# Six attentions make their scores twice, the second time with keys on the partitions

## What is computed

```python
# L0_attn, L2_attn: heads of 8, causal (L0 with rotary positions)
scores = q @ k.T / sqrt(8); scores = where(tril, scores, -inf); o = softmax(scores) @ v
# L1_xattn: heads of 8, 77 keys from the context, no mask;  L3_ffn: heads of 8, no mask
# L2_xattn = two attentions with heads of 32: a1 (128 keys) and a2 (77 keys of the context)
a = softmax(q @ k.T * 32 ** -0.5)
if causal: a = a * (arange(t)[None, :] > arange(s)[:, None])   # a1 only, AFTER the softmax
o = a @ v
```

## Time and profile before

| | us |
|---|---|
| median of 3 runs | 4947.15 |
| lowest, highest | 4937.4, 4949.03 |
| the profiled execution, span from its first to its last instruction | 4969.4 |

### The profile page before, as it was taken

How to read it: one execution, slowest core, us unless ns; L and a number is a source line. 1 busy time by engine, 2 the same in 40 slices (tenths; PEclk the granted TensorE clock), 3 DMA queues, 4 the chain that set the end, 5 groups by cost and what they waited for, 6 DMA issues and landing times.

```text
span 4969.4 us, 84778 instructions
## 1 busy us (share of the span) xinstructions
PE 4410.3 (89%) x29077; PEld 2535.4 (51%) x29077; DVE 2640.3 (53%) x6880; ACT 2593.2 (52%) x9813; POOL 836.2 (17%) x1454
## 2 busy tenths in 40 slices
PE   7888989989999999989799888998889888898796
PEld 3544764444454454448355444454455454554493
DVE  5555225655655655645454656556664565546523
ACT  4556434454454454453555556555655566555542
POOL 0111420011011011035021021110131021210350
PEclk9999989999999999999899989999999999999897
DMA  5000540000000000007000000000000000000172
GB/s 198 11 11 11 172 128 18 12 7 28 12 7 28 12 7 18 6 22 222 22 22 10 5 5 24 14 10 1 6 23 14 9 6 10 10 1 1 46 230 76
DMA packets 107750, 183.05 MB, mean 37 GB/s; under 512 B 13344, under 2 KB 69408, under 8 KB 107200
## 3 DMA queue, kind: packets, MB, share of 16 engines
q1 hardware_dynamic: 92544, 147.48, 9.9%
q0 software_dynamic: 13632, 28.04, 1.6%
q10 hardware_dynamic: 1152, 2.10, 0.1%
HBM read 126.33 MB, written 51.23 MB: 36 GB/s over the span
## 4 chain that ended last, share of the span: by engine, by line
PE 65%; DVE 20%; ACT 7%; issue 5%; DMA 2%; POOL 1%; SPq 0%; DVEq 0%; POOLq 0%; ACTq 0%
PE bank L713 8%; PE bank L866 7%; PE bank L883 6%; DVE rowmax L1693 6%; PE bank L745 4%; PE bank L1041 3%; PE bank L733 3%; PE bank L1152 3%; PE bank L1141 3%; PE bank L1023 3%; PE bank L790 3%; DVE probsT L1759 2%; PE bank L922 2%; PE bank L852 2%; ACT work L1323 2%
## 5 line engine op out<-in xcount | busy, mean ns | idle before, releaser
L1323 ACT ACTIVATE work<-bank,rowmax 128x128 f32<-128x128 f32 (+1 forms) x3072 | 1061.1, 398 | 208.6 <-DVE rowmax L1693 208.6
L1693 DVE TENSOR_REDUCE rowmax<-bank 128x4 f32<-128x512 f32 (+2 forms) x1152 | 614.0, 578 | 433.4 <-PE bank L866 314.8
L713 PE MATMUL bank<-mask_causal,identb 128*128 128x512 bf16 x2839 | 803.1, 394 | 22.6 <-DVE qd L1628 8.7
L883 PE MATMUL bank<-ident,work 128*128 128x128 f32 (+1 forms) x4096 | 641.0, 282 | 155.6 <-DVE probsT L1759 116.7
L1323 ACT ACTIVATION_READ_ACCUMULATOR work<-bank,rowmax 128x1 f32 x3072 | 753.1, 245 | 0.0
L883 PEld LDWEIGHTS bank<-ident,work 128*128 128x128 f32 (+1 forms) x4096 | 481.8, 144 | 377.7 <-DVE probsT L1759 196.8
L1759 DVE COPY probsT<-bank 128x512 f32<-128x512 f32 (+2 forms) x832 | 482.0, 601 | 55.3 <-PE bank L883 53.9
L713 PEld LDWEIGHTS bank<-mask_causal,identb 128*128 128x128 bf16 x2839 | 273.5, 101 | 290.7 <-issue 115.5
L866 PE MATMUL bank<-km,q 32*128 32x512 f32 (+2 forms) x1792 | 403.7, 562 | 1.9 <-issue 1.9
L2206 POOL TENSOR_TENSOR qd<-work 128x256 f32<-128x256 f32 (+1 forms) x64 | 64.7, 1012 | 1902.9 <-ACT work L1321 1836.5
L1257 ACT ACTIVATE part<-bank,eps 128x512 f32<-128x512 f32 x232 | 157.7, 680 | 383.8 <-PE bank L745 383.3
(11 more groups left out here) (336 smaller groups left out, 6902.5 us busy)
## 6 DMA issues: line engine op xcount, KB each, us to landing
slot<-in_w_L_ffn SPq DMA_DIRECT2D x78, 578.0 KB
slot<-in_w_stream SPq DMA_DIRECT2D x41, 512.0 KB
expert_rows<-slot SPq DMA_DIRECT2D x36, 516.0 KB, 6.3
slot<-in_w_L_ffn SPq DMA_DIRECT2D x39, 450.0 KB
qd<-expert_rows SPq DMA_DIRECT2D x117, 129.0 KB
back<-pair_rows SPq DMA_DIRECT2D x24, 512.0 KB, 5.3
slot<-in_w_stream SPq DMA_DIRECT2D x16, 256.0 KB
pair_rows<-qd,dest POOLq DMA_INDIRECT x234
```

Source lines behind the costliest of these rows:

```text
L713: nc.tensor.matmul(b[:], identb[:], mask["causal"][:].unsqueeze(1).to_broadcast([P, 4, P]), start=True, stop=True)
L883: ins = nc.tensor.transpose(b[0:nk, j * P:(j + 1) * P], probs[t % 2][:, r, j, 0:nk], ident[:])
L1323: ins = nc.scalar.activation(out, raw, ACT.Exp, bias=top, accum_out=expsum[t % 2][:, 4 * r + j:4 * r + j + 1])
L1693: V.tensor_reduce(m[:, 4 * r:4 * r + J], banks.where(("scores", n, c, s, r))[:, 0:J * nk] .rearrange("p (j k) -> p j k", j=J), AX_X, ALU.m ...
```

## The change

Six attentions (`KEYED`) get functions of their own, `keyed_mha`. The scores with queries on the partitions now serve the maxima alone. The negative maxima of an item, 16 columns, are split into two bf16 parts (value and remainder), laid out in `tops` and turned by one matmul. The scores are made a second time with keys on the partitions, and a matmul with a 0/1 weight (`top_pick`) adds each query's negative maximum to them in the bank. One exponential per block then gives `probsT` directly; nothing is turned. The sums come from matmuls with weights of ones (`totals`), already spread over the features; ScalarE inverts them by logarithm and exponential. In `L2_a1` the late mask is multiplied into a copy of `probsT` (in `probs`), blocks 0 and 1 by VectorE, 2 and 3 by GpSimd. Rings: `first` (banks 0 to 2) and `second` (3 to 5). `after_mask` becomes bf16, `average64` goes (the narrower variance is scaled in the logarithm), two small constants come in, `xcol` shares memory with `lcol`.

```diff
+KEYED = ("L0_attn", "L1_xattn", "L2_attn", "L2_a1", "L2_a2", "L3_ffn",)
+FRONT_ROWS, BACK_ROWS = (0, 1), (2, 3)
...
         banks = Banks(psum, {"flow": range(8), "scores": (0, 1, 2, 3), "turned": (4, 5), "attend": (6,), "wide": (7,),
-                             "head": (4, 5)})
+                             "head": (4, 5), "first": (0, 1, 2), "second": (3, 4, 5)})
...
+            # TensorE
+            def half(t, rows):
+                back = BACK_ROWS if rows == FRONT_ROWS else FRONT_ROWS
+                if t < GROUP:                               # (waits for q, k at s == 0)
+                    for r in rows:
+                        b = bank(("scores", n, c, s, r), ("row_max", (n, c, s, r)), "first")
+                        if st["mask"]: # identity x mask, 4 * nk columns bf16
+                if 1 <= t <= GROUP:                         # c, s = items[t - 1]
+                    for r in back:
+                        b = bank(("keyed", n, c, s, r), ("probsT", (n, c, s, r)), "second")
+                        if st["mask"]: # mask x identity, 512 columns bf16
+                for j in range(4):
+                    # scores of t: D == 32 one matmul of nk columns per r in rows; else at j == 0 one of 4 * nk
+                    # keyed of t-1: per r in back one matmul, keys x queries, 128 columns, stop=False
+            def turn_tops(t): # bank "first"; waits tops; one matmul tops x identb
+            def shift(t, rows):
+                if rows == BACK_ROWS:
+                    pe.wait_ge(*have("tops_taken", (n, c, s)))
+                for j in range(4):
+                    for r in rows:  # top_pick[g32, j] spread over nk x topsT[g32], 128 columns bf16, into keyed
+            def totals(t): # bank "wide", freed by log_sum; waits probsT of all r; 16 matmuls of 128 columns fp32
+            for t in range(GROUP + 2):
+                if t == GROUP + 1: step(then)
+                if t == 0: warm(6, "second")
+                half(t, FRONT_ROWS)
+                if 1 <= t <= GROUP: turn_tops(t - 1)
+                if t >= 2: totals(t - 2)
+                elif t == 1: warm(4, "second")
+                if 1 <= t <= GROUP: shift(t - 1, BACK_ROWS)
+                half(t, BACK_ROWS)
+                if 1 <= t <= GROUP: shift(t - 1, FRONT_ROWS)
+                # hooks of second; step(late[0]); attend(t - 2), in L2_a1 after kept_v, kept_p; output
+            # ScalarE, round t: take_tops(t - 1), soften(t - 1), invert(t - 2)
+            def soften(t):
+                for r in BACK_ROWS + FRONT_ROWS:
+                    act.wait_ge(*have("keyed", (n, c, s, r)))
+                    nc.scalar.activation(probsT..., banks.where(("keyed", n, c, s, r))..., ACT.Exp).then_inc(*made("probsT", (n, c, s, r)))
+            def invert(t): # waits summed; Ln from the bank -> log_sum; Exp(-1 x) -> inverse
+            # VectorE
+            for t in range(GROUP + 2):
+                if t < GROUP: row_max(t, FRONT_ROWS)
+                if st["post"] and t >= 2: keep_before(t - 2)   # probs = probsT * after_mask, r = 0, 1
+                if t >= 3: context(t - 3)
+                if t < GROUP:
+                    row_max(t, BACK_ROWS)
+                    split_tops(t)                              # two small steps
+                # hooks, late steps; at GROUP + 1 context(t - 2); add_residual
+            # GpSimd, L2_a1: the same product for r = 2, 3
```

More of the change, by code:

```diff
@@ L477, in decoder @@
         spreadT = [sb(f"spreadT{i}", [P, 4, P]) for i in range(2)]
+        tops = sb("tops", [P, P], BF16)
+        topsT = sb("topsT", [P, P], BF16)
         diag = [B["y"][c][:, 0:PER * 32].rearrange("p (s i) -> p s i", s=PER) for c in C]
@@ L547, in _ @@
                 nc.gpsimd.memset(onesb[:], 1.0)
+                nc.gpsimd.memset(tops[:], 0.0)
                 nc.gpsimd.memset(slots[SLOTS - 1][:], 0.0)
@@ L567, in _ @@
                 nc.vector.memset(wmean[:], 0.0)
-                nc.vector.memset(average64[:], 1.0 / CTX_DIM)
                 for value, t in eps.items():
@@ L668, in norm_rings, with keyed, top_cols @@
             return "flow", "flow"
+        def keyed(st):
+            return untagged(st["name"])[0] in KEYED
+        def top_cols(part):
+            return tops[:].rearrange("p (r x) -> p r x", r=4)[:, :, 0:8] \
+                .rearrange("p r (j i) -> p r j i", i=2)[:, :, :, part]
         def summed_by_pool(st, r):
-            return not st["linear"] and not st["mask"] and r in POOL_SUMS
+            return not st["linear"] and not st["mask"] and not keyed(st) and r in POOL_SUMS
         def per_feature(st):
@@ L744, in variance @@
                     pe.wait_ge(*have("squared", (n, c)))
-                    nc.tensor.matmul(b[0:rows, 0:w], (average if rows == P else average64)[:],
+                    nc.tensor.matmul(b[0:rows, 0:w], average[0:rows, 0:rows],
                                      B["sq"][c][0:rows, 0:w],
@@ L817, in mha @@
                 def mha(st, second, then):
+                    if keyed(st):
+                        keyed_mha(st, second, then)
+                        return
                     n, nk, D = st["name"], st["nk"], st["D"]
@@ L1300, in mha_head, with keyed_mha, take_tops @@
                     yield
+                def keyed_mha(st, second, then):
+                    n, nk, D = st["name"], st["nk"], st["D"]
+                    def take_tops(t):
+                        c, s = items[t]
+                        act.wait_ge(*have("tops_turned", (n, c, s)))
+                        nc.scalar.activation(topsT[:], banks.where(("tops_turned", n, c, s))[:, 0:P],
+                                             ACT.Copy).then_inc(*made("tops_taken", (n, c, s)))
+                    def soften(t):
+                        c, s = items[t]
+                        if t >= 2:
+                            act.wait_ge(*have("attended", (n, *items[t - 2])))
+                        for r in BACK_ROWS + FRONT_ROWS:
+                            act.wait_ge(*have("keyed", (n, c, s, r)))
+                            nc.scalar.activation(probsT[t % 2][0:nk, r, :, :], banks.where(("keyed", n, c, s, r))[0:nk, :]
+                                                 .rearrange("p (j t) -> p j t", j=4),
+                                                 ACT.Exp).then_inc(*made("probsT", (n, c, s, r)))
+                    def invert(t):
+                        c, s = items[t]
+                        w = 4 if D == 32 else 1
+                        out = spreadT[t % 2][:, 0:w, :]
+                        if t == 0 and untagged(n)[0] == "L2_a1" and st["group"]:
+                            for i in C:
+                                act.wait_ge(*have(f"scattered{i}", (tagged("L3_route", st["group"] - 1), i, 1, PER - 1)))
+                        if t >= 2:
+                            act.wait_ge(*have("context", (n, *items[t - 2])))
+                        act.wait_ge(*have("summed", (n, c, s)))
+                        nc.scalar.activation(out, banks.where(("summed", n, c, s))[:, 0:w * P].rearrange("p (i t) -> p i t", i=w),
+                                             ACT.Ln, scale=float(P) if D == 32 else 1.0).then_inc(*made("log_sum", (n, c, s)))
+                        act.wait_ge(*have("log_sum", (n, c, s)))
+                        nc.scalar.activation(out, out, ACT.Exp, scale=-1.0).then_inc(*made("inverse", (n, c, s)))
+                    for t in range(GROUP + 2):
+                        if 1 <= t <= GROUP:
+                            take_tops(t - 1)
+                            soften(t - 1)
+                        if t >= 2:
+                            invert(t - 2)
+                        for _ in range(st["hooks"].count(t)):
+                            step(second)
+                        if t == st["drained"]:
+                            drain(second)
+                        if t:
+                            step(late[0])
+                        if t == PER + 1 and untagged(n)[0] == "L3_ffn":
+                            g = st["group"]
+                            for c in C:
+                                act.wait_ge(*input_of(("normed", tagged("L3_xattn_ln", g)), c))
+                                act.dma_start(io["kept"][:, (g * CHAINS + c) * TOK:(g * CHAINS + c + 1) * TOK], B[st["src"]][c][:]
+                                              ).then_inc(*made(f"kept{c}", (g, c), 16))
+                        if t == GROUP + 1:
+                            step(then)
+                            step(then)
```

221 lines of the change are left out of this document (216 added, 5 removed).

## The result

The changed kernel takes 5186.35 us in the median (5156.61 to 5190.27, 4 runs) against 4948.09 for the kernel before in the same comparison: ratio 1.0464, 95% interval 1.0428 to 1.0499. It is slower by 4.6%, where 4915 and a gain were forecast. The profiled execution has a span of 5184.5 us against 4969.4.

A forecast was written before the change was run, and what follows sets the result against it. TensorE, busy 89% of the span, was taken as the bound. Six attentions -55 us, moved wait +22, setup under 0.5: sum -32, span 4969 to 4937; the median, 22 us below the span, gives 4915 us, range 4800 to 5045.

The forecast's parts named there:

- TensorE's round: TensorE's time for one round of a keyed attention: 5.9 us unmasked, 7.2 us masked.
- the halves: In each round, scores and the previous item's keyed scores run beside each other on different row groups, 1.0 us a half.
- the wait for the fourth bank: TensorE idles after the first shift until ScalarE's exponential frees the first block's bank: 0.95 us, only 0.2 in masked items.
- the count's wait: In six masked attentions the routing's count waits for bank `wide` behind ScalarE's logarithm: 1.8 us twice in each, +22 us.
- rival E: Idle time lets TensorE's clock fall to 1.2 GHz in 13 of 128 unmasked rounds: +63, 4978 us; chance 0.05.
- removed fillers and turns: Taken out of TensorE's round: sixteen turns (1.75 us of slots) and all fillers between turns (up to 1.3 us).
- C's middle: Rival C, slower halves: each 0.1 us more costs 38 us, 5049 us at 1.35, 5299 fully serial; chance 0.15.

The follow-up runs named there:

- split: Changed kernel with half of the totals issued behind the back shift in unmasked keyed attentions: 5141.73 us, 1.0232 of the kernel before.
- Experiments 1 to 3 and 7 to 9: fill77; changed kernel's 77-key stages with 128 key columns, 1.0444; tall77; fill77's fillers on 32 rows, 1.0135; unmasked totals and attend on 77 rows, 1.0512; before_bare.
- tall77: Changed kernel with totals and attend of L1_xattn and L2_a2 reading 128 rows instead of 77: 5096.37 us, 1.0145 of the kernel before.
- fill77: Changed kernel with fillers in L1_xattn and L2_a2, six in round 0 and four in each later round: 4973.66 us, 1.0041 of the kernel before.
- before_bare: Kernel before the change without its fillers in L1_xattn and L2_a2: 4940.28 us, 0.9972 of the kernel before.
- early_128: Changed kernel keying only the four 128-key attentions, masked ones inverting totals between back and front exponentials: 1.0018 of the kernel before.
- three_fill: Changed kernel keying only L2_a1, L2_a2 and L3_ffn, with fillers in L2_a2 (six in round 0, four a round): 0.9925 of the kernel before.

## Why the prediction was wrong

- **TensorE's round, the halves, the wait for the fourth bank, the count's wait:** right, each within 0.15 us (5.85 for 5.9, 7.05 for 7.2, 0.83 for 0.95, 1.84 for 1.8), and split showed the wait by removing half of it.
- **The step that failed is the clock: the sum took full speed in every round, and rival E, the fall, was given 5 in 100 and priced at +63.** Its "against" read: in two items of `L3_ffn` TensorE is busy for 10.09 of 12.50 us, as idle as the new round, and was granted 1.00. That took the busy share for what the clock follows, and one stage for all six. Experiments 1 to 3 and 7 to 9 show otherwise: the same keyed `L1_xattn` at 0.50 in three groups and at 1.00 in one, where it is 88% busy, the bare old form at 1.00 with 86%, and the level moved by rows fed alone (tall77). The Trainium skill (TensorE: Matmul & The Clock Gate, Part 1, "What's actually happening") has the clock set by how busy the engine has been; these windows agree only if busy is not read as the profile's busy share.
- **The price:** at most 13 rounds at the low level were assumed. It was seven stages of eight, each with four or five rounds near 9.7 instead of 5.8 us and parts of others, and in `L2_a2` the projections of the second chain with them. Their place (229 us in the stretches of `L1_xattn` and `L2_a2`, -2 predicted) is nearly the whole miss: 4915 + 231 = 5146, and `L2_a1`'s 15 too few make 5161 of the measured 5186. With the clock held (fill77) the same stretches are at +26 and -8, so 211 of the 231 are the clock. For the last 24, the forecast counted the median 22 us under the profiled execution, while here the two are 2 us apart.
- **What was taken out:** I named removed fillers and turns only as time. They also fed TensorE 128 rows at a time; nothing in the sum asked what a stage that feeds 77 and 32 rows would be granted. In the old form the fillers were not needed for it (before_bare); that the turns were is likely, but no run took them out alone.
- **Size at full clock:** with the clock held (fill77 against before, stage by stage) `L1_xattn` costs 26 us, not 14, and `L2_a2` brings 8, not 16; `L2_a1` brought 29, not 44. The settled rounds are right, so the rest lies in the first and last ones. In `L2_a1` about 8 of the 15 us are the clock again, at its entry: a round of 8.88 and one of 8.84 us in the third and fourth group, and the longer ones ahead of them.
- **The range** ended at 5045, on C's middle. With E's own price of 4.9 us a round on all 64 rounds of the eight 77-key stages it would have had to reach 4915 + 314 = 5229.

What stays open is the exact measure by which the chip grants the clock. Shown is: more rows fed bring it back and fewer delay its return, fillers of 128 rows hold it and fillers of 32 mostly do, more weight columns do not, a smaller gap alone mostly does not, and a stage of 77 keys keeps the level that it has after two or three rounds until a different kind of work comes. Rows may not be all of it: with the projections of the second chain, matmuls of 128 and of 64 rows, TensorE was busy for 17 of 17 us at 0.50.

## What to carry to other kernels

Where a change replaces full-height matmuls (turns, fillers) by ones that feed part of the array, price the stage at both clock levels and look at what feeds TensorE just before it; a busy share like that of a fast stage is no proof. Six full-height fillers at the entry of such stages held six of eight here, where one of eight had held without them. And key only where the old round was longer than the new one and no other stage waits for a bank that is now freed later: the masked round fell from 7.34 to 7.05 us and the masked attentions lost all the same, by the count's wait. Three of the six attentions, with split totals and those fillers in `L2_a2`, made a kernel 1.6% faster, all six as they were one 4.6% slower.

## What was not expected of the hardware

- **Two levels for one program:** `L1_xattn` ran at 5.73 us a round in one group and 9.70 in the other three of the same execution, with busy shares of 88% and 92%.
- **Chips differ where GpSimd issues indirect DMAs.** On two of the chips the kernel before took 5019 us instead of 4955. There instructions of TensorE and ScalarE come late while GpSimd issues the routing's indirect DMAs, which it does on the other chips too; early_128, second hosted count, TensorE and then ScalarE:

```profile
204.26 1.21 PE L1075 MATMUL bank<-probsT,small 128*32 128x128 f32 x31
205.79 0.27 PE L1075 MATMUL bank<-probsT,small 128*32 128x128 f32 x1 [0.32 <-issue]
206.10 0.69 PE L1056 MATMUL bank<-topsT,top_pick 32*128 32x128 bf16 x8
207.21 0.59 PE L1005 MATMUL bank<-mask_causal,identb 128*128 128x512 bf16 x2 [0.42 <-issue]
...
210.29 0.39 PE L1012 MATMUL bank<-identb,mask_causal 128*128 128x512 bf16 x1 [2.27 <-ACT probsT L1487]
```

```profile
209.63 1.08 ACT L1487 ACTIVATE probsT<-bank 128x512 f32<-128x512 f32 x2 [3.58 <-remote]
```

The last record of the totals starts 0.32 us after the others have ended, released by nothing that the profile shows. ScalarE's exponentials start 2.8 us after the shift that they need has ended (206.79), and TensorE waits 2.27 us for them. Why the instructions come late is not shown. From the first count on, three rounds of the keyed masked form take some 12 us more than on the other chips (18.1 and 10.3 us instead of 9.84 and 6.60 in tall77), those of the old form some 7 (10.9, 11.4 and 6.1 instead of 8.66, 7.18 and 5.45 in three_fill and the kernel before).
